# The first of the two rounding subtractions of the gated FFN values, on GpSimd instead of VectorE

## What is computed

```python
def fp4_quant_dequant(x):                      # along the last dim, blocks of 16
    scale = max(abs(xb)) / 6.0, at least 1e-12
    xn = xb / scale
    idx = searchsorted(_MID, abs(xn))          # nearest of 0, .5, 1, 1.5, 2, 3, 4, 6
    q = _GRID[idx] * sign(xn) * scale

gate = fp4_linear(x, w_gate)                   # w_gate (352, 128)
y = fp4_linear(x, w_up)                        # w_up (352, 128)
h = silu(gate) * y
return fp4_linear(h, w_down)                   # w_down (128, 352)

x = x + attention(layernorm(x))
x = x + ffn(layernorm(x))
```

## Time and profile before

| | us |
|---|---|
| median of 3 runs | 1351.75 (1350.59 to 1353.01) |
| the profiled execution | 1352.66 |
| its span in the trace | 1350.8 |
| busy in the span | PE 1269.7, DVE 855.6, ACT 890.6, POOL 1054.3 |
| granted TensorE clock, mean | 0.976 of full speed |

### The profile page before, as it was taken

How to read it: one execution, slowest core, us unless ns; L and a number is a source line. 1 busy time by engine, 2 the same in 40 slices (tenths; PEclk the granted TensorE clock), 3 DMA queues, 4 the chain that set the end, 5 groups by cost and what they waited for, 6 DMA issues and landing times.

```text
span 1350.8 us, 24752 instructions
## 1 busy us (share of the span) xinstructions
PE 1269.7 (94%) x7429; PEld 667.8 (49%) x7429; DVE 855.6 (63%) x2350; ACT 890.6 (66%) x1272; POOL 1054.3 (78%) x457
## 2 busy tenths in 40 slices
PE   4999999999999999999999999999999998888566
PEld 3555555555455555555454555555555554443245
DVE  6656666656566556666566555666656667786694
ACT  4767667777676677676677667767667766654243
POOL 4488888898788888888888888888898888779142
PEclk9999999999999999999999999999999999899687
DMA  2000000000000000000000000000000000000001
GB/s 63 2 9 2 1 2 10 1 1 2 3 10 1 2 1 9 2 1 2 5 7 2 1 1 9 2 2 1 4 1 1 1 2 1 2 1 1 0 1 32
DMA packets 45951, 6.66 MB, mean 5 GB/s; under 512 B 37344, under 2 KB 45664, under 8 KB 45808
## 3 DMA queue, kind: packets, MB, share of 16 engines
q1 hardware_dynamic: 45584, 4.41, 2.6%
q0 software_dynamic: 224, 0.54, 0.1%
HBM read 3.75 MB, written 1.05 MB: 4 GB/s over the span
## 4 chain that ended last, share of the span: by engine, by line
PE 84%; DVE 7%; issue 5%; POOL 2%; ACT 1%; DMA 0%; POOLq 0%; SPq 0%; DVEq 0%; ACTq 0%
PE o_ps L1180 32%; PE s_ps L1028 24%; PE mx_ps L1050 8%; PE mx_ps L1043 4%; PE misc_ps L1170 3%; PE misc_ps L1162 2%; PE misc_ps L1015 2%; PE misc_ps L993 2%; PE s_ps L1036 1%; PE misc_ps L994 1%; PE misc_ps L995 1%; POOL acc_pool L508 1%; PE s_ps L1270 1%; DVE split L743 1%; PE misc_ps L999 1%
## 5 line engine op out<-in xcount | busy, mean ns | idle before, releaser
L508 POOL TENSOR_TENSOR acc_pool<-acc_pool,probs 128x1024 f32<-128x1024 f32 x352 | 853.3, 2424 | 49.7 <-POOL acc_pool L508 41.6
L625 ACT ACTIVATE probs<-s_ps 128x1024 f32<-128x1024 f32 x512 | 525.5, 1027 | 70.5 <-PE s_ps L1028 29.2
L797 DVE CUSTOM_DVE_ANT_0 summed<-mx_ps,rise 128x512 bf16<-128x512 f32 x503 | 344.8, 686 | 331.5 <-issue 290.6
L1180 PE MATMUL o_ps<-probs,vv 128*64 128x512 f32 x2048 | 498.6, 607 | 6.1 <-ACT probs L625 6.1
L545 ACT ACTIVATE rise<-mx_ps 128x512 f32<-128x512 f32 x503 | 300.0, 596 | 270.4 <-PE mx_ps L1043 258.5
L1180 PEld LDWEIGHTS o_ps<-probs,vv 128*64 128x64 f32 x2048 | 127.0, 136 | 223.0 <-issue 179.6
L1043 PE MATMUL mx_ps<-k_raw,q_hi 64*128 64x512 f32 x503 | 224.0, 445 | 9.1 <-DVE part_max L797 7.9
L1050 PE MATMUL mx_ps<-k_hi,q_hi 64*128 64x512 f32 x503 | 223.6, 445 | 7.4 <-issue 3.6
L1028 PE MATMUL s_ps<-q_hi,k_hi 64*128 64x512 f32 x1024 | 205.7, 395 | 0.9 <-ACT probs L625 0.8
L1028 PE MATMUL s_ps<-q_hi,k_lo 64*128 64x512 f32 x1024 | 203.9, 392 | 0.0
L1028 PE MATMUL s_ps<-q_lo,k_hi 64*128 64x512 f32 x1024 | 203.7, 391 | 0.0
(11 more groups left out here) (160 smaller groups left out, 1098.1 us busy)
## 6 DMA issues: line engine op xcount, KB each, us to landing
mrow<-neg_max SPq DMA_DIRECT2D x256, 0.5 KB, 2.0
wqkv<-in_L_attn_w_qkv SPq DMA_DIRECT2D x8, 192.0 KB, 2.8
y<-in_L_attn_x SPq DMA_DIRECT2D x4, 256.0 KB, 4.4
out<-y SPq DMA_DIRECT2D x4, 256.0 KB, 2.3
wo<-in_L_attn_w_out SPq DMA_DIRECT2D x8, 64.0 KB, 1.9
wx<-in_L_ffn_w_down POOLq DMA_DIRECT2D x1, 176.0 KB, 6.2
wx<-in_L_ffn_w_gate POOLq DMA_DIRECT2D x1, 128.0 KB, 4.5
wx<-in_L_ffn_w_up POOLq DMA_DIRECT2D x1, 128.0 KB, 5.1
```

The costliest lines, as they stand in the source:

```text
L508: pool.tensor_tensor(acc, first, probs[:, j % P_BUFS, :, :], ALU.add) \
L625: act.activation(probs[:, j % P_BUFS, :, :], s_ps[:, j % 2, :, :], ACT.Exp, scale=SCALE) \
L797: dve.tensor_tensor_reduce(summed[:, s % 2, :], mx_bank(h, pair), rise[:, h, :], 1.0, LOWEST, ALU.add, ALU.max, part_max[:, slot:slot + 1] ...
L1180: ins = pe.matmul(o_ps[DH * h:DH * (h + 1), :], vv[par(w)][:, j, DH * h:DH * (h + 1)], probs[:, j % P_BUFS, h, :], start=(j == 0), stop=(j ...
```

## The change

GpSimd gets step 1 of the rounding for numbers 5 to 8: `rest_of(n)`, which waits for VectorE's step 0 (semaphore `f_split`), subtracts in place, and raises `f_rest`. VectorE's step 1 becomes a wait for `f_rest`. While numbers 7 and 8 are made, steps 1 and 2 of the tensor that is two behind now both stand after the third `hidden` call, and nothing stands after the second.

```diff
-POOL_ORDER = [("times", 3), ("over", 4), ("over", 5), ("times", 4), ("over", 6), ("times", 5), ("over", 7),
-              ("times", 6), ("over", 8), ("times", 7), ("times", 8)]
+POOL_ORDER = [("times", 3), ("over", 4), ("over", 5), ("times", 4), ("over", 6), ("rest", 5), ("times", 5), ("over", 7),
+              ("rest", 6), ("times", 6), ("over", 8), ("rest", 7), ("times", 7), ("rest", 8), ("times", 8)]
+FIRST_H = 5
@@
+            def rest_of(n):
+                width = quantised(n)[2]
+                a, c = scaled[buf(n)][:, 0:width], split[buf(n)][:, 0:width]
+                pool.wait_ge(f_split, n - FIRST_H + 1)
+                pool.tensor_tensor(a, c, a, ALU.subtract).then_inc(f_rest, 1)
@@
                 if k == 0:
                     dve.wait_ge(f_abs, n + 1)
-                    inc(dve.tensor_scalar(c, a, SPLIT, SPLIT, ALU.mult, ALU.max))
+                    ins = dve.tensor_scalar(c, a, SPLIT, SPLIT, ALU.mult, ALU.max)
+                    if n >= FIRST_H:
+                        ins.then_inc(f_split, 1)
+                    else:
+                        inc(ins)
+                elif k == 1 and n >= FIRST_H:
+                    dve.wait_ge(f_rest, n - FIRST_H + 1)
                 elif k == 1:
                     settle()
                     inc(dve.tensor_tensor(a, c, a, ALU.subtract))
@@
                     if g:
-                        grid_step(h - 2, k)
+                        for m in ((k,) if h - 2 < FIRST_H else ((0,), (), (1, 2), (3,))[k]):
+                            grid_step(h - 2, m)
```

More of the change, by code:

```diff
@@ L293, in block_kernel @@
         f_abs = sem("f_abs")
+        f_split = sem("f_split")
+        f_rest = sem("f_rest")
         f_grid = sem("f_grid")
@@ L520, in _ @@
             body(ITERS - 1, True)
-            for what, n in POOL_ORDER:
-                over_scale(n) if what == "over" else times_scale(n)
+            def rest_of(n):
[3 more added lines that the diff above has]
+                pool.tensor_tensor(a, c, a, ALU.subtract).then_inc(f_rest, 1)
+            for what, n in POOL_ORDER:
+                if what == "over":
+                    over_scale(n)
+                elif what == "rest":
+                    rest_of(n)
+                else:
+                    times_scale(n)
         @block.scalar
```

## The result

| | before | changed |
|---|---|---|
| median us | 1351.83 (1350.54 to 1353.01, 6 runs) | 1358.63 (1355.8 to 1362.34, 6 runs) |
| ratio | 1 | 1.0054, 95% interval 1.004 to 1.0069 |
| span of the profiled execution | 1350.8 | 1356.5 |

The changed kernel is slower by 6.8 us between medians, 5.4 to 9.3 by the interval. It lies in the range, above the forecast of 1357.1.

The account below looks back on a forecast made before the run. VectorE was taken to bound the stretches rounding numbers 5 and 6, then a chain from engine to engine the tail. Delays of 2.04 and 3.30 us gave +5.3 on 1351.75, so 1357.1 us, range 1354.3 to 1359.4.

Parts of the forecast that it names:

- R: Time of the new GpSimd subtraction of 1408 columns, taken as 3.20 us from adds reading two full f32 operands.
- The block multiply's 2.59: Rival: the GpSimd subtraction takes only 2.59 us, like the same-width multiply by block scales; +2.9 us, 1354.7; chance 0.09.
- the spacing's 3.38: Rival: the GpSimd subtraction takes 3.38 us, from the start-to-start spacing of two adds; +6.1 us, 1357.9; chance 0.12.
- Handovers: Around the new subtraction: 0.09 us from VectorE to GpSimd and 0.05 to the next engine, 0.14 together.
- The middle stretches: Where numbers 5 and 6 are rounded: second subtraction 1.02 us later each, all passed on, 2.04 us together.
- Absorption: Rival: the stretches of numbers 5 and 6 absorb their delay, only the tail pays; +3.3 us, 1355.1; chance 0.06.
- The tail: Where numbers 7 and 8 are rounded: second subtraction 1.65 us later each, both counting, 3.30 us together.
- Sum of these: Delays of numbers 5 to 8 together: 4R - 7.46, +5.3 us with R = 3.20.
- The clock: TensorE's granted speed near the end: +1.4 us at 0.5, -0.3 at full speed; no case or chance, only in the range.
- The signs: What the changed profile would show, including `finish(0)` 2.0 us later, `finish(1)` 3.7 and `finish(2)` 5.3.
- 2.04: Not-slower rival: R must be under 2.04 to gain in the middle stretches, under 1.87 for the sum; chance 0.05.
- The two-operand hold: Rival: the new subtraction holds VectorE's `hidden` call, another 0.46 us in two stretches; +6.3 us, 1358.0; chance 0.04.

Follow-up runs that it names:

- the half width: Changed kernel with the new GpSimd subtraction on the first 704 of 1408 columns only, the rest left out: 1352.34 us, ratio 0.9993 to the kernel before.
- the middle alone: Kernel before with the subtraction moved to GpSimd for numbers 5 and 6 only, 7 and 8 staying on VectorE: 1356.07 us, ratio 1.0024.
- the shared version: Changed kernel with GpSimd subtracting the first 704 columns and VectorE the other 704, steps in their old slots: 1355.44 us, ratio 1.0021.
- the third profile of before: Kernel before, unchanged, profiled a third time: 1353.01 us, one run.
- the second profile of before: Kernel before, unchanged, profiled a second time: 1352.34 us, one run.
- the filled kernel before: Kernel before with 12, 16, 16 and 30 unread transposes ahead of four entries of TensorE's queue: 1350.3 us, ratio 0.9985.

## Why the prediction was right, and where it was short

**R.** 3.20 from the two adds' rows, 3.16 measured; the half width gave 1.67 against 1.68 from the same line. The block multiply's 2.59 and the spacing's 3.38 are out as values of R.

**Handovers.** 0.14 forecast, 0.11 measured (0.08 to GpSimd and 0.03 from it).

**The middle stretches.** 1.02 each forecast, 0.97 measured, and passed on in full: shown by the middle alone. Absorption is out. What VectorE was relieved of became idle time, since its next instruction for the tensor needs the subtraction's result; the two `hidden` calls fill 0.94 of the wait, as worked out.

**The tail.** 1.65 each forecast, 1.57 measured on VectorE and GpSimd (1.61 from finish to finish at full clock).

**Sum of these.** 5.34 forecast, 2 x 0.97 + 2 x 1.57 = 5.1 measured.

**The clock, the term that was missing.** The text said that the clock in the tail might shift the sum either way and gave it no case; only the upper end of the range had 1.4 for it, and with that the range held. It went one way: 1.1 to 1.5 us on average over the profiles. 5.1 and that make 6.2 to 6.6, beside 6.8 between medians. The mistake is in how I read the tail stage, from one profile. Its 1.64 and 1.47 us were themselves a mix of two levels, so there was 0.6 to 0.8 a stage to lose and only 0.2 to 0.3 to win (1.31 at full speed). From the earlier trace rows I took a stretch behind the last finish but one, which changed little (6.1 and 6.0 us against 5.7, 6.15 and 5.8), instead of the two behind the waits that grow.

**The signs.** Counted from the reciprocal of number 5, `finish(0)` came 1.95 us later, `finish(1)` 4.16 and `finish(2)` 6.55, where 2.0, 3.7 and 5.3 were forecast. The excess begins where the clock term does.

**Two slips that change nothing.** A gain in the middle stretches would begin at R under 2.18, by the prediction's own R-2.18; its 2.04 takes the handovers off twice. And the cases that it counts as slower by over 0.2% add up to 0.9, not 0.88.

**The two-operand hold.** Chance 0.04 for `hidden` being held: it was not, but an instruction with two SBUF operands would have been, as the shared version shows.

**What stays open.** What decides the level. The middle alone had the lower one in both tail stages with waits of the old length, and so had one of six stages of before. TensorE had been idle for 2.2 us ahead of the lower level in the third profile of before and for 5.6 in the changed kernel, but for 3.6 ahead of full speed in the second profile of before, so the last idle time by itself does not decide. The clock's share of the difference thus rests on ten stages on either side, in few executions.

## What to carry to other kernels

Moving an instruction off the busiest engine helps only if something independent can run while the other engine works at it. Compare the distance from its input to its consumer, handovers included, before and after, and not the sums of busy time. In a chain from engine to engine every added microsecond counts once for each pass. A chain's TensorE part should be priced at both clock levels, since one kernel can get either. Read a stage of that kind from more than one profile.

## What the runs showed of the hardware

A stage of nine small f32 matmuls (1.31 us at full clock, 2.28 at half) takes either value in executions of one and the same kernel. Transposes of the identity into an unused bank, issued while TensorE waits, kept the level behind `times_scale` at 0.98 to 1.00 and gained 4 us in stages of the changed kernel and 2.0 us of the whole kernel before. They do not hold it everywhere: the filled kernel before was at 0.52 for 6 us behind `finish(1)`. GpSimd's span beside a VectorE instruction that holds it grows in the record itself: 1.68 us became 2.38, so a GpSimd duration read from a busy stretch may include a wait.
